# An expert stage with fewer of its slots written out on TensorE and ScalarE, and more of them run by the loop

## The reference

```python
x = x + layernorm(recurrence(layernorm(x)))
h = layernorm(x)                       # 4096 tokens x 128
scores = sigmoid(h @ gate_w.T)         # 32 experts
ids = top_k(scores + e_bias, 4)        # 4 of 32
w = scores[ids] / sum(scores[ids])
g, u = h @ w1[e], h @ w3[e]            # 128 -> 96, for each chosen expert
out = sum over chosen e of w_e * (silu(g) * u) @ w2[e]
x = x + layernorm(out)
```

## Time and profile before

| what | us |
|---|---|
| median of 3 runs (lowest, highest) | 341.75 (341.36, 342.93) |
| the profiled execution's own time | 343.86 |
| its span in the profile | 342.1 |
| PE busy in the span | 283.5 (83%) |
| DVE, ACT, POOL busy | 257.1, 217.8, 236.2 |
| expert stage, first half (TensorE) | from 112.98 to 180.17 |
| expert stage, second half (TensorE) | from 180.17 to about 244 |

### The profile page before, as it was taken

One profiled execution on the slowest core, in us unless ns is written; L12 is line 12 of the kernel. 1 busy time (PEld: TensorE's weight loads), 2 busy tenths in 40 slices (PEclk: granted clock), 3 DMA queues, 4 the chain that ended last, 5 costly groups with the idle time before them and its releaser, 6 DMA issues.

```text
span 342.1 us, 6589 instructions
## 1 busy us (share of the span) xinstructions
PE 283.5 (83%) x1515; PEld 224.0 (65%) x1516; DVE 257.1 (75%) x976; ACT 217.8 (64%) x546; POOL 236.2 (69%) x272
## 2 busy tenths in 40 slices
PE   4575687587674999999998989999999999999760
PEld 2244254454453889889886988888776766898540
DVE  3878679878989477787448978744578887867796
ACT  6938766988683555556554555555588678765672
POOL 4395777777777777777743777777777777777700
PEclk9965666866965699999999999999999999999995
DMA  3999999961111556667646999876511121521222
GB/s 98 313 306 287 280 279 281 307 172 51 47 54 55 155 161 197 185 198 223 200 140 172 250 253 268 236 206 179 148 52 53 47 54 49 141 59 52 67 77 61
DMA packets 83999, 54.81 MB, mean 160 GB/s; under 512 B 8032, under 2 KB 80512, under 8 KB 83968
## 3 DMA queue, kind: packets, MB, share of 16 engines
q1 hardware_dynamic: 57472, 30.85, 33.1%
q0 software_dynamic: 6912, 14.17, 14.5%
q10 hardware_dynamic: 19584, 9.44, 9.8%
HBM read 25.07 MB, written 29.36 MB: 159 GB/s over the span
## 4 chain that ended last, share of the span: by engine, by line
PE 38%; POOL 17%; DVE 13%; ACT 11%; issue 11%; DMA 5%; SPq 4%; POOLq 0%; ACTq 0%; DVEq 0%
POOL xs_dram L404 17%; PE bank L1676 6%; PE bank L1667 6%; PE bank L1672 6%; PE bank L1594 4%; PE bank L1626 3%; SPq L305 3%; DMA xb<-xs_dram 3%; PE bank L1462 3%; PE bank L1495 2%; PE bank L1607 2%; PE bank L1589 2%; PE bank L1455 2%; ACT L460 2%; DVE at_at L1351 1%
## 5 line engine op out<-in xcount | busy, mean ns | idle before, releaser
L413 POOL DMA_INDIRECT yk<-ys_dram,row_ys x108 | 107.4, 994 | 41.5 <-issue 26.8
L404 POOL DMA_INDIRECT xs_dram<-xn_all,row_xs x108 | 108.6, 1006 | 36.2 <-issue 32.3
L1594 PE MATMUL bank<-w,xbT 128*128 x288 | 60.5, 333 | 0.3 <-ACT xbT L617 0.2
L617 ACT COPY xbT<-bank 128x256 f32<-128x256 f32 x72 | 26.8, 373 | 33.1 <-PE bank L1589 29.7
L1092 DVE TENSOR_TENSOR act_a<-silu,bank 128x192 f32<-128x192 f32 x72 | 25.4, 353 | 29.9 <-ACT silu L620 26.2
L1594 PEld LDWEIGHTS bank<-w,xbT 128*128 128x128 f32 x288 | 46.0, 194 | 1.1 <-issue 0.9
L1626 PE MATMUL bank<-w2s,aT 96*128 x288 | 46.0, 282 | 0.1
L1626 PEld LDWEIGHTS bank<-w2s,aT 96*128 96x128 f32 x288 | 37.7, 191 | 2.4 <-issue 1.4
L1676 PE MATMUL bank<-at_at,xn_all 128*128 128x384 f32 (+1 forms) x96 | 34.8, 444 | 4.0 <-DVE at_at L1351 3.9
L1101 DVE COPY yb<-bank 128x256 f32<-128x256 f32 x72 | 30.4, 422 | 8.5 <-PE bank L1626 6.8
L620 ACT ACTIVATE silu<-bank 128x192 f32<-128x192 f32 x72 | 23.8, 331 | 20.1 <-PE bank L1594 19.4
(11 more groups left out here) (216 smaller groups left out, 532.8 us busy)
## 6 DMA issues: line engine op xcount, KB each, us to landing
xb<-xs_dram SPq DMA_DIRECT2D x144, 64.0 KB
ys_dram<-yb ACTq DMA_DIRECT2D x72, 128.0 KB, 2.6
xs_dram<-zeros SPq DMA_DIRECT2D x2, 2048.0 KB, 15.0
ys_dram<-zeros SPq DMA_DIRECT2D x1, 2816.0 KB, 13.4
ys_dram<-zeros SPq DMA_DIRECT2D x1, 2560.0 KB, 18.2
x_sb<-in_L_attn_x_dram SPq DMA_DIRECT2D x8, 256.0 KB, 5.8
xs_dram<-xn_all,row_xs POOLq DMA_INDIRECT x108
yk<-ys_dram,row_ys POOLq DMA_INDIRECT x108, 2.5
```

The lines of the kernel that those rows point to most:

```text
L404: pool.indirect_dma_start(out=xs[h], out_offset=bass.IndirectOffsetOnAxis(ap=row_xs[:, j, k:k + 1], axis=0), in_=xn2_all[:, j, :], in_offs ...
L413: pool.indirect_dma_start(out=yk[h][:, j - h * TP, k, :], out_offset=None, in_=ys[h], in_offset=bass.IndirectOffsetOnAxis(ap=row_ys[:, j, ...
L617: act.copy(xbT[:, p, :, :].rearrange("c b t -> c (b t)"), ps_xbT[p][:, 0:2 * P]).then_inc(b_xc[h], 1)
L1594: ins = pe.matmul(ps_gu[o][:, b * 2 * I:(b + 1) * 2 * I].rearrange("t (w a i) -> t w a i", w=2, a=1), xbT[:, o, b, :], w13[:, :, bass.ds(e ...
```

## The change

TensorE writes out 16 slots of the first half and 12 of the second, ScalarE 16 and 8; VectorE still writes out 24 of each, and SyncE's loop is as before. The slots that are no longer written out are done by the loop: on TensorE it goes round five times in the first half and six in the second, on ScalarE five and seven times (before, three). The second half's number of steps is read between the last written-out slot of the first half and its loop, after slot 15, where before it was read at slot 20; VectorE still reads it at slot 20.

```diff
     FIXED = [(-(-n * K // SLOTS) - 1) * BODY for n in TH]
+
+    PE_FIXED, ACT_FIXED = [4 * BODY, 3 * BODY], [4 * BODY, 2 * BODY]
...
             for h in range(HALVES):
-                for t in range(FIXED[h]):
-                    if h == 0 and t == 20:
-                        most.append(steps_value(act, 1))
+                for t in range(ACT_FIXED[h]):
                     slot(h, t, t % BODY, stages(t))
                     if h == 0:
                         late(t)
-                with act.Fori(FIXED[h] // BODY - 1, most[h] + 2) as q:
+                if h == 0:
+                    most.append(steps_value(act, 1))
+                with act.Fori(ACT_FIXED[h] // BODY - 1, most[h] + 2) as q:
...
             for h in range(HALVES):
-                for t in range(FIXED[h]):
-                    if h == 0 and t == 20:
-                        most.append(steps_value(pe, 1))
+                for t in range(PE_FIXED[h]):
                     if h and t == 3:
                         wait_apart(pe, b_yc[0], most[0] * BODY + 3 * BODY)
                     slot(h, t, t // BODY, t % BODY, stages(t))
-                with pe.Fori(FIXED[h] // BODY - 1, most[h] + 2) as q:
+                if h == 0:
+                    most.append(steps_value(pe, 1))
+                with pe.Fori(PE_FIXED[h] // BODY - 1, most[h] + 2) as q:
```

## The result

The changed kernel takes 345.02 us in the median of 9 runs (343.66 to 346.63), the kernel before 342.84 in 9 runs beside it (341.36 to 343.93). The ratio is 1.0064, 95% interval 1.0041 to 1.0087: slower by 2.2 us, with 1.4 to 3.0 in the interval. The forecast was +2.7, or 344.5 us.

What follows compares the result with a forecast made beforehand. The prediction took TensorE to bound the kernel: 1.0 us passed on from the first half plus 1.7 from the second gave +2.7 on the median of 341.75, so 344.5 us, with a range of 341.3 to 347.0.

Steps and rivals of the forecast that it cites:

- TensorE is the bound, ScalarE is not: Expert stage: time lost by TensorE's queue shows in the total, time lost by ScalarE's mostly doesn't; ScalarE's term was nothing.
- ScalarE's share of the high end: ScalarE's six more rounds: if uncovered, six branches of 0.25 us, 1.5 us in all, counted only in the high end.
- A round behind a back edge costs 6.89 to 7.31, taken as 7.1: TensorE's looped rounds of four slots: 7.1 us each after a taken branch, against 6.15 without any stall.
- First half +1.2: TensorE from slot 16 to the first half's end: 35.1 us against 33.9, with 0.1 to 2.2 us more possible.
- the read of the steps: TensorE's read of the number of steps, now after slot 15 of the first half: 0.4 us, between 0 and 0.75.
- Second half +1.7: TensorE from slot 12 to the second half's end: 41.7 us against 40.0, with 0.9 to 2.6 us more possible.
- All but 0.2 of the first half's delay arrives: Between the halves: the first half's delay passes on through VectorE's work and the block loads, 1.0 of 1.2 us.
- The rival in which all is swallowed: Between the halves: waits for scatters and slot 10's block hide the first half's delay, leaving +1.7 us, 343.5; chance 0.15.
- a gap at slot 10 that is gone: Second half: TensorE's wait for slot 10's block, 0.92 us before, vanishing was listed as a sign the prediction was wrong.
- Only the branch is paid: TensorE's loops: the queue keeps its lead, each of five back edges costs 0.33 us, giving 342.6 us; chance 0.12.
- Faster through late blocks: Second half: late blocks at slots 10, 16 and 20 come free, giving -1.8 us, 340.0; chance 0.10.
- Refetching the body: TensorE's loops: each back edge fetches the loop's body again by DMA, five giving +22 us, 364; chance 0.02.

Runs made afterwards that it cites:

- e2: ScalarE alone changed (16 and 8 slots written out) against the kernel before, TensorE 24 and 24, steps read ahead of the loop: 343.01 us, ratio 1.0008.
- e5: The changed kernel with one TensorE load of four registers at the end of every second slot: 341.32 us, ratio 0.9953 to the kernel before.
- e4: TensorE's second half alone changed (12 slots written out, 24 in the first) against the kernel before, steps read ahead of the loop: 345.32 us, ratio 1.0069.
- e1: TensorE alone changed (16 and 12 slots written out) against the kernel before, ScalarE 24 and 24: 345.83 us, ratio 1.0085.
- e3: TensorE's first half alone changed (16 slots written out, 24 in the second) against the kernel before, ScalarE 24 and 24: 344.27 us, ratio 1.0042.
- e6: The kernel before with one TensorE load of four registers at the end of every second slot: 339.90 us, ratio 0.9906 to the kernel before.
- e7: The changed kernel with its four loads of two registers each moved to the end of its slot: 349.34 us, ratio 1.0176 to the kernel before.

## Why the prediction was right, and where it was only near

- **TensorE is the bound, ScalarE is not.** Right: e2 at +0.3 us. ScalarE's share of the high end, six branches of 0.25 us, was too dear by itself: each took 0.05.
- **A round behind a back edge costs 6.89 to 7.31, taken as 7.1.** The nine measured average 6.96: the mechanism right, the middle 0.14 too high. Nearly the whole loss lies in the first slot behind the branch, and e5 shows that it hangs on the register loads. The branch with its register work was taken as 0.33 and holds the queue for 0.45. The seven rounds that were priced at 7.1, 49.7 us together, took 48.9: 0.8 too much.
- **First half +1.2.** +1.4 in the changed kernel's profile, 1.7 in the mean of three against three. The term that was too small is the read of the steps: taken as 0.4, measured 7.16 - 6.49 = 0.67 in the changed kernel and 0.5 to 0.8 in e2 and e4. I had read it off the lateness at slot 20, where it stood in straight code. Why it costs more ahead of the loop was not taken apart.
- **Second half +1.7.** +1.5 in the changed kernel's profile, 2.1 in the mean of three against three. The back edges were cheaper and the entry round dearer (7.05 in place of 6.46), as the late block came at slot 12, the start of that round, where it had been at slot 10, and uncovered the register load behind it. The prediction had no term for that: it took 6.46 for any round entered from straight code, and in e1 and e4 the one at slot 12 took 7.57 and 7.71. So the near hit of this term is in part luck; errors of 0.6 and 0.8 us went against each other.
- **All but 0.2 of the first half's delay arrives.** Right in kind, e3 +1.4 (0.7 to 2.2); the path goes through VectorE's work between the halves, as the prediction said. In the changed kernel's profile the stage is 1.57 us longer up to the start of the second half and 1.23 up to its slot 12, a loss of 0.3. The rival in which all is swallowed fell. The prediction's sign against itself, a gap at slot 10 that is gone, did come, but it comes in e2 and e4 too and tells nothing of the first half.
- **Sum +2.7** against 2.2 measured, 1.4 to 3.0. In the profile the stage grew by 2.8. That 344.5 us lies only 0.5 under the 345.02 is in part luck: the kernel before took 342.84 in the nine runs beside it, 1.1 more than the 341.75 that the sum was put on, and that made up for the half microsecond by which the sum was too high, and more.
- **Only the branch is paid** fell: with a load in every slot a round behind a back edge takes 0.8 more than the stall-free 6.15, with half of the loads 0.2 in the mean and nothing in the best rounds.
- **Faster through late blocks** fell: the block that is late moved from slot 10 to slot 12 and cost 0.98 in place of 0.92 us of idle time, and a slot of 2.35 us behind it.
- **Refetching the body** fell: no round of the changed kernel took more than 7.26, and TensorE's instruction transfers on the page of the profile (queue q8, which is TensorE's by e1 with 9 packets and e2 with 12) went down from 12 packets to 9 with nine taken branches. The Trainium skill's rule in "Runtime: NRT & Kernel Launch", Instruction fetch mechanics, speaks of targets outside the two pages at hand; no run here shows a fetch for this body of four slots.

## What to carry to other kernels

A branch in a loop is paid from the lead that an engine's queue has over its engine. Ask how much lead a round gains (here 0.09 us in a slot, for a branch that holds the queue for 0.45 and uncovers the load behind it) before asking what a branch costs; if the lead is short, thin out the register loads and read several slots' numbers at once, and only then argue about how much to unroll. A wait for late data costs more than itself in the same way, in straight code too, so fewer register loads also pay there. The lead itself is nowhere measured: it is worked out from the queue's times and from what e5 and e6 did.

## What the runs showed of the hardware that was not expected

Loading four registers from SBUF with one instruction took 0.36 us in the median of e5 and 0.44 in that of e6 (0.33 at least) on TensorE's queue, loading two 0.54 (0.53 at least); not a price per register, at any rate. The same load of two at the end of a slot took 0.63 in the median (e7). Of the branches on that queue the one that ends a loop took 0.08 us and the taken ones 0.21 to 0.25; on ScalarE's queue they took 0.045 to 0.055. The Trainium skill, "Advanced Engine Details and Errata", Control Flow Timing, gives about 108 ns for a compare-and-branch: half of what TensorE's took when taken and twice what ScalarE's did. In the 6.15 us rounds of e5 nothing of the branch was seen in the time.
